# Attention's product of probabilities and values in four 32-column groups of the array, partial sums added when y is read

## The reference

```python
q = _apply_rope(q, cos, sin); k = _apply_rope(k, cos, sin)
scores = jnp.einsum('bhqd,bhkd->bhqk', q, k) / jnp.sqrt(jnp.asarray(hd, x.dtype))
scores = jnp.where(causal, scores, jnp.asarray(-jnp.inf, x.dtype))
attn = jax.nn.softmax(scores, axis=-1)
y = jnp.einsum('bhqk,bhkd->bhqd', attn, v)
...
return jnp.einsum('btc,oc->bto', y, w_proj)
```

## Time and profile before

| | |
|---|---|
| time, median of 3 runs | 3512.9 us (3508.41 to 3513.11) |
| span of the profiled execution, first to last instruction | 3506.6 us |
| loop over heads within it | from about 2785 to 3316 us |
| period of a head in the steady state | 16.00 us (3003.76 to 3019.76) |
| mean granted clock of TensorE, whole span | 0.954 |

### The profile page before, as it was taken

How to read it: one execution, slowest core, us unless ns; L and a number is a source line. 1 busy time by engine, 2 the same in 40 slices (tenths; PEclk the granted TensorE clock), 3 DMA queues, 4 the chain that set the end, 5 groups by cost and what they waited for, 6 DMA issues and landing times. The chain is left out here.

```text
span 3506.6 us, 40196 instructions
## 1 busy us (share of the span) xinstructions
PE 3137.1 (89%) x11856; PEld 1686.1 (48%) x11856; DVE 2278.1 (65%) x3726; ACT 1005.0 (29%) x2369; POOL 660.5 (19%) x441
## 2 busy tenths in 40 slices
PE   2899899988989989899898998988799799999989
PEld 1444454444544445444454454544684433333368
DVE  4777777777777777776777767665546455555354
ACT  1322323223232232232222322322213233333321
POOL 1122122122222212212222221222210000000021
PEclk7899999999999999999999999998899899999999
DMA  5000010010010001001001100000104100000000
GB/s 169 13 22 4 25 49 13 1 65 19 4 59 25 4 25 50 13 1 65 19 4 56 28 4 19 33 0 1 64 0 166 50 28 22 27 22 27 9 7 18
DMA packets 48126, 107.68 MB, mean 31 GB/s; under 512 B 9104, under 2 KB 18400, under 8 KB 45248
## 3 DMA queue, kind: packets, MB, share of 16 engines
q1 hardware_dynamic: 42624, 102.47, 8.8%
q10 hardware_dynamic: 5312, 2.92, 0.3%
HBM read 86.23 MB, written 19.14 MB: 30 GB/s over the span
## 5 line engine op out<-in xcount | busy, mean ns | idle before, releaser
L439 PE MATMUL bank<-xnT,wh 128*128 128x512 f32 x1280 | 592.4, 607 | 124.4 <-DVE sg L842 92.2
L528 PE MATMUL bank<-wg,xnT 128*128 128x512 f32 x1024 | 482.3, 615 | 0.0
L580 PE MATMUL bank<-wo,ggT 128*128 128x512 f32 x1024 | 466.0, 609 | 0.5 <-ACT ggT L689 0.5
L439 PEld LDWEIGHTS bank<-xnT,wh 128*128 128x128 f32 x1280 | 241.2, 194 | 410.8 <-issue 278.1
L733 DVE SCALAR_TENSOR_TENSOR cacc<-raw,cwh,cacc 128x512 f32<-128x512 f32 x480 | 390.3, 813 | 17.0
L580 PEld LDWEIGHTS bank<-wo,ggT 128*128 128x128 f32 x1024 | 201.7, 198 | 237.7 <-issue 232.3
L1821 PE MATMUL bank<-at_PT,at_vz 128*49 128x512 f32 (+3 forms) x768 | 298.5, 499 | 0.8 <-ACT at_yTs L1890 0.8
L528 PEld LDWEIGHTS bank<-wg,xnT 128*128 128x128 f32 x1024 | 193.4, 199 | 197.3 <-issue 197.3
L1914 DVE TENSOR_REDUCE at_nm<-bank 128x1 f32<-128x512 f32 (+3 forms) x256 | 151.1, 591 | 206.4 <-PE bank L1783 161.8
L503 PEld LDWEIGHTS bank<-xch,em 128*128 128x128 f32 x2048 | 237.4, 194 | 55.2 <-issue 52.2
L503 PE MATMUL bank<-xch,em 128*128 128x64 f32 x2048 | 243.5, 278 | 6.4 <-DVE em L791 2.4
(11 more groups left out here) (243 smaller groups left out, 4655.3 us busy)
## 6 DMA issues: line engine op xcount, KB each, us to landing
wh<-w_hs_dram SPq DMA_DIRECT2D x80, 256.0 KB, 2.7
wg<-w_gate_dram SPq DMA_DIRECT2D x8, 2048.0 KB, 7.7
wo<-w_out_dram SPq DMA_DIRECT2D x8, 2048.0 KB, 8.7
qk_scratch<-at_part SPq DMA_DIRECT2D x48, 256.0 KB
at_qT<-qk_scratch SPq DMA_DIRECT2D x32, 192.0 KB, 2.6
at_kT<-qk_scratch SPq DMA_DIRECT2D x32, 192.0 KB, 2.6
pk<-pack_scratch SPq DMA_DIRECT2D x16, 272.0 KB, 3.1
wgu<-w_gu_dram SPq DMA_DIRECT2D x1, 3584.0 KB, 11.3
```

Source lines behind the costliest of these rows:

```text
L439: mm = nc.tensor.matmul(BA[bank][:, :], wh[:, j, k, :], xnT[:, k, h * HALF:(h + 1) * HALF], start=(k == 0), stop=(k == KC - 1))
L528: mm = nc.tensor.matmul(BA[b][:, :], xnT[:, k, ttok], wg[:, k, u * 512:(u + 1) * 512], start=(k == 0), stop=(k == KC - 1))
L580: mm = nc.tensor.matmul(BA[b][:, :], ggT[:, j, :], wo[:, j, :], start=(j == 0), stop=(j == JT - 1))
```

## The change

`vz` loses its zeros on the left: it holds 17 columns and 15 of zeros, and the stationary operand has 32 columns. Each of the 12 products is written to one of four groups of 32 partitions of `BYT` (g = 0 to 3), which are four groups of 32 columns of the array. Groups 0, 1 and 2 share the products of b = 1, group 3 has those of b = 0. ScalarE copies all 128 partitions, the transposes bring all four groups along, and VectorE adds the three partial sums of b = 1 when it reads them. The products stand in three runs of four, behind `s1(., 2)`, `s1(., 4)` and `s1(., 6)`; nothing of them is left behind `s1(., 7)` or `m_rows`.

```diff
-            vz = sb(c1, "at_vz", [P, 2, NT, VZ + AD + 1 + VZ])
+            vz = sb(c1, "at_vz", [P, 2, NT, VZ])
             yT_ = sb(c1, "at_yTs", [P, T // 2])
+            yp = sb(c1, "at_yp", [P, NT, AD + 1])
...
-                    nc.gpsimd.memset(yT_[:, :], 0.0).then_inc(s_set, 1)
-                    pool.wait_ge(s_set, 4)
+                    pool.wait_ge(s_set, 3)
...
-                            lo = 0 if b else VZ
-                            mm = nc.tensor.matmul(BYT[0:VZ + AD + 1, 512 - n:], vz[:, r, j, lo:lo + VZ + AD + 1], PT_[:, r, c:c + n],
-                                                  start=((b, j) == PV1[0]), stop=((b, j) == PV3[-1]))
+                            mm = nc.tensor.matmul(BYT[VZ * g:VZ * (g + 1), 512 - n:], vz[:, r, j, :], PT_[:, r, c:c + n],
+                                                  start=((g, b, j) in OPENS), stop=((g, b, j) in ENDS))
...
-                    PV1 = [(1, 0), (1, 7), (1, 6), (1, 5), (1, 4), (1, 3)]
-                    PV2 = [(1, 2), (1, 1)]
-                    PV3 = [(0, 0), (0, 1), (0, 2), (0, 3)]
-                    AMONG = {1: 0, 2: 1, 3: 2, 4: 3, 5: 4, 6: 5}
+                    PV1 = [(0, 1, 0), (1, 1, 1), (2, 1, 3), (3, 0, 0)]
+                    PV2 = [(0, 1, 5), (1, 1, 2), (2, 1, 4), (3, 0, 1)]
+                    PV3 = [(0, 1, 6), (1, 1, 7), (3, 0, 2), (3, 0, 3)]
+                    OPENS = PV1
+                    ENDS = [(0, 1, 6), (1, 1, 7), (2, 1, 4), (3, 0, 3)]
+                    AMONG = {2: PV1, 4: PV2, 6: PV3}
...
                             if before and i in AMONG:
-                                b, j = PV1[AMONG[i]]
-                                pv(h - 1, 1 - r, b, [j])
+                                pv(h - 1, 1 - r, AMONG[i])
...
-                        if before:
-                            for b, j in PV2:
-                                pv(h - 1, 1 - r, b, [j])
                         if not last:
                             m_rows(h + 1, 1 - r)
-                        if before:
-                            for b, j in PV3:
-                                pv(h - 1, 1 - r, b, [j])
...
-                        nc.scalar.copy(yT_[0:VZ + AD + 1, :], BYT[0:VZ + AD + 1, :]).then_inc(a_y.sem, 1)
+                        nc.scalar.copy(yT_[:, :], BYT[:, :]).then_inc(a_y.sem, 1)
...
-                        ps = BM[:, :].rearrange("p (i s d) -> p s i d", i=NT // 2, s=P // VZ)[:, 0:2]
-                        nc.vector.reciprocal(ri[:, :].rearrange("p (s i) -> p s i", s=2), ps[:, :, :, AD]).then_inc(v_ri.sem, 1)
-                        v_ri.wait(dve, h + 1)
-                        nc.vector.tensor_tensor(halves(yo[:, :, :]), ps[:, :, :, 0:AD],
-                                                halves(ri[:, :].unsqueeze(2).broadcast_to([P, NT, AD])), ALU.mult).then_inc(v_y.sem, 1)
+                        ps = BM[:, :].rearrange("p (i s d) -> p i s d", i=NT // 2, s=P // VZ)
+                        nc.vector.tensor_copy(yp[:, 0:NT // 2, :], ps[:, :, 3, 0:AD + 1]).then_inc(v_ri.sem, 1)
+                        nc.vector.tensor_reduce(yp[:, NT // 2:, :], ps[:, :, 0:3, 0:AD + 1].rearrange("p i s d -> p i d s"),
+                                                AX, ALU.add).then_inc(v_ri.sem, 1)
+                        v_ri.wait(dve, 3 * h + 2)
+                        nc.vector.reciprocal(ri[:, :], yp[:, :, AD]).then_inc(v_ri.sem, 1)
+                        v_ri.wait(dve, 3 * h + 3)
+                        nc.vector.tensor_tensor(yo[:, :, :], yp[:, :, 0:AD],
+                                                ri[:, :].unsqueeze(2).broadcast_to([P, NT, AD]), ALU.mult).then_inc(v_y.sem, 1)
```

More of the change, by code:

```diff
@@ L1758, in _ @@
                     nc.gpsimd.memset(vz[:, :, :, :], 0.0).then_inc(s_set, 1)
-                    nc.gpsimd.memset(yT_[:, :], 0.0).then_inc(s_set, 1)
-                    pool.wait_ge(s_set, 4)
+                    pool.wait_ge(s_set, 3)
                     def take(h, r):
                         t_pv.wait(pool, h - 1)
-                        nc.gpsimd.tensor_copy(vz[:, r, :, VZ:VZ + AD + 1], V[:, :, bass.ds(h, 1), :].rearrange("p z o d -> p z (o d)"))\
+                        nc.gpsimd.tensor_copy(vz[:, r, :, 0:AD + 1], V[:, :, bass.ds(h, 1), :].rearrange("p z o d -> p z (o d)"))\
                             .then_inc(po_v.sem, 1)
@@ L1808, in m_rows, with pv @@
                         mm.then_inc(t_m.sem, 1)
-                    def pv(h, r, b, js):
-                        for j in js:
-                            if (b, j) == PV1[0]:
+                    def pv(h, r, blocks):
+                        for g, b, j in blocks:
+                            if (g, b, j) == PV1[0]:
                                 po_v.wait(pe, h + 1)
@@ L1819, in pv @@
                             c = OFF[j] + q0_ - j * P
-                            lo = 0 if b else VZ
-                            mm = nc.tensor.matmul(BYT[0:VZ + AD + 1, 512 - n:], vz[:, r, j, lo:lo + VZ + AD + 1], PT_[:, r, c:c + n],
-                                                  start=((b, j) == PV1[0]), stop=((b, j) == PV3[-1]))
-                            if (b, j) == PV3[-1]:
+                            mm = nc.tensor.matmul(BYT[VZ * g:VZ * (g + 1), 512 - n:], vz[:, r, j, :], PT_[:, r, c:c + n],
+                                                  start=((g, b, j) in OPENS), stop=((g, b, j) in ENDS))
+                            if (g, b, j) == PV3[-1]:
                                 mm.then_inc(t_pv.sem, 1)
-                    PV1 = [(1, 0), (1, 7), (1, 6), (1, 5), (1, 4), (1, 3)]
-                    PV2 = [(1, 2), (1, 1)]
-                    PV3 = [(0, 0), (0, 1), (0, 2), (0, 3)]
-                    AMONG = {1: 0, 2: 1, 3: 2, 4: 3, 5: 4, 6: 5}
+                    PV1 = [(0, 1, 0), (1, 1, 1), (2, 1, 3), (3, 0, 0)]
[4 more added lines that the diff above has]
+                    AMONG = {2: PV1, 4: PV2, 6: PV3}
                     def turn(h):
@@ L1854, in body @@
                             if before and i in AMONG:
-                                b, j = PV1[AMONG[i]]
-                                pv(h - 1, 1 - r, b, [j])
+                                pv(h - 1, 1 - r, AMONG[i])
                             if i == 2 and (not isinstance(h, int) or h >= 2):
                                 turn(h - 2)
-                        if before:
-                            for b, j in PV2:
-                                pv(h - 1, 1 - r, b, [j])
                         if not last:
                             m_rows(h + 1, 1 - r)
-                        if before:
-                            for b, j in PV3:
-                                pv(h - 1, 1 - r, b, [j])
                     def last(h, r):
                         body(h, r, True)
-                        for b, j in PV1 + PV2 + PV3:
-                            pv(h, r, b, [j])
+                        pv(h, r, PV1 + PV2 + PV3)
                         turn(h - 1)
@@ L1900, in last @@
                         take_y(h)
-                    act.wait_ge(s_set, 4)
+                    act.wait_ge(s_set, 3)
                     heads(act, None, body, last, (a_ex, a_y))
@@ L1933, in output @@
                         t_y.wait(dve, h + 1)
-                        ps = BM[:, :].rearrange("p (i s d) -> p s i d", i=NT // 2, s=P // VZ)[:, 0:2]
-                        halves = lambda ap: ap.rearrange("p (s i) d -> p s i d", s=2)
-                        nc.vector.reciprocal(ri[:, :].rearrange("p (s i) -> p s i", s=2), ps[:, :, :, AD]).then_inc(v_ri.sem, 1)
-                        v_ri.wait(dve, h + 1)
-                        nc.vector.tensor_tensor(halves(yo[:, :, :]), ps[:, :, :, 0:AD],
-                                                halves(ri[:, :].unsqueeze(2).broadcast_to([P, NT, AD])), ALU.mult).then_inc(v_y.sem, 1)
+                        ps = BM[:, :].rearrange("p (i s d) -> p i s d", i=NT // 2, s=P // VZ)
[7 more added lines that the diff above has]
+                                                ri[:, :].unsqueeze(2).broadcast_to([P, NT, AD]), ALU.mult).then_inc(v_y.sem, 1)
                         v_y.wait(dve, 2 * h + 1)
```

## The result

The changed kernel takes 3531.9 us (median of 4 runs, 3528.2 to 3535.3) against 3512.6 us before (median of 4 runs too): 1.0058 of the time, with a 95% interval of 1.0043 to 1.0072. It is slower, as forecast, but by 19 us and not by 67. Its profiled execution has a span of 3533.0 us.

The account below looks back on a forecast made before the run. TensorE sets the period, with a latency chain covered by products. A head of 16.7 us plus 1.6 for the clock is 18.3, against 16.00; 31 x 2.3 = +71, less 2.8 and 1.7, gives +67: 3580 us, range 3500 to 3630.

Parts of the forecast that it names:

- What bounds the kernel: Steady head: TensorE, busy 15.58 of 16.00 us, sets the period, plus a VectorE latency chain at the end covered by products.
- the price of a product: Single product between scores: 1.14 us, of which 0.853 product, about 0.06 mask matmul, 0.23 way in and out.
- the bubble: Head's end, last s1 to next s2: 4.03 us chain through VectorE, bare of products after the change.
- The waits behind it: TensorE behind VectorE's longer output: 0.42 us for s1(3)'s maximum, 0.7 us for s1(4)'s maxima and two banks.
- What the groups give: A head's three runs of products: 4.90 us in place of 7.68, bounds 2.35 and 7.68.
- staircase: Within a run, only one product's second pass overlaps the next's first: four 512-column products take 5 passes, 2.13 us.
- Rival 1: All four products of a run abreast, clock drops partly hidden: 16.3 us a head, 3515 us; chance 0.18.
- The clock: At bare head ends granted clock drops to 1.2 GHz in 8 of 10, 2.0 us each: 1.6 us a head.
- rival 3: Two-pass staircase as forecast, no clock drops: 16.7 us a head, 3530 us; chance 0.13.
- The order's price: Per head, 3.0 us of bubble that held products and 1.6 us of stalls, outweighing gains of 2.78 and 1.15 us.
- The signs: Whole kernel's time: chance of faster by over 0.2% 0.17, same 0.07, slower 0.76.
- The ways in and out: Around each run of products TensorE pays 0.23 us once; the range allowed for this doubled, 3545 to 3610 us.

Follow-up runs that it names:

- e1_busy_end: Changed kernel with ten idle bfloat16 matmuls of 512 columns ahead of the 8 transposes at each head's end: 3466.1 us, 0.9873 of before.
- e9_pairs_adjacent: e1_busy_end with products of one group placed next to each other in the first two runs of products: 3498.7 us, 0.9962 of before.
- e3_new_order_49: Kernel before with only its products reordered into the changed kernel's three runs of four, 49 columns wide, no groups: 3664.3 us, 1.0431 of before.
- e6: Changed kernel with second and third runs of products back at the head's end and VectorE's output moved earlier: 3401.9 us, 0.9689 of before.
- e2_runs_at_end: Changed kernel with second and third runs of products moved back to the head's end, around the transposes: 3479.9 us, 0.9909 of before.
- e8_end_early_busy: e6 plus five idle bfloat16 matmuls of 512 columns between the second run of products and the 8 transposes: 3414.9 us, 0.9721 of before.

## Why the prediction failed, point by point

**What bounds the kernel, the price of a product, the bubble: right.** The end of the head without products was put at 4.03 us and is 4.10 (3014.94 to 3019.04). The output on VectorE was put at 1.55 us and takes 1.42 (3009.61 to 3011.03 in this trace). The waits behind it were put at 0.42 and 0.7 us, and are 0.29, 0.41 and 0.45. The wait for the exponentials was put at 0.5 us and is 0.45 in e1_busy_end, at full clock.

**What the groups give: wrong, and this is the step that failed.** "The trace shows matmuls start in program order, never one ahead of another" was true of a trace in which the products share columns of the array (all 76 matmuls of the head from 3003.76 stand in program order), and it cannot tell what happens when they don't. I took 4.90 us for the products of a head. No run shows this staircase or its 4.90 us; the runs show 2.35 in streams: in e1_busy_end, at full clock, the three runs take 1.00, 0.99 and 0.78 us from their start to the next matmul (3005.93 to 3006.93, 3009.20 to 3010.19, 3012.83 to 3013.61), of which 0.14 each is the way out. e9_pairs_adjacent shows what happens in its place: only a matmul's own group held it back. 2.55 us a head, 79 us over 31 heads, is more than the whole error of 48 us. The lower bound of 2.35 us stood in the text; the choice between the bounds went by the wrong row. Rival 1, a run at the cost of its widest product, was nearer to what happens: the four groups here, in float32, give 3.2 times (3.14 us in e3_new_order_49 for 0.99). Across groups matmuls do not start strictly in order: in e9 the first product of one group begins with the first of the other (3008.32 and 3008.31), ahead of three passes that stand before it.

**The clock: right in kind, too small in size.** I read head 0 as the model of every head and took a fall in 8 of 10, 1.6 us a head. It falls in every head of the profiled stretch, and e1 measures what it costs: 17.07 - 14.82 = 2.25 us a head, 66 us in all. This undid a part of the first error, and the sum can be redone: from the forecast head of 18.3 us, 2.55 us less of products, 0.7 more of waits and 0.65 more by the clock give 17.1, and 17.07 was measured. Over 31 heads that is 38 of the 48 us; of the other 10 the last head makes 5.5, put at 2.8 us of gain and measured at 8.3. At full clock the head was predicted at 14.8 us if the groups run side by side; e1 has 14.82 (3003.38 to 3018.20).

**So after is rival 1, whose place was right and whose number was not**: 14.8 us and a fall, put at 16.3 us and 3515 us since I thought a part of the fall hidden in waits for VectorE; it is 17.07 and 3532. That rival 3 stood at 3530 is chance: its period of 16.7 us had the staircase and no falls, and neither is in the trace.

**The order's price** of "3.0 us of bubble that held products and 1.6 us of stalls" can be read off the runs: e3, the order alone, is 152 us; moving the two runs back and the output out of the way (e6) takes 130 us from the changed kernel.

**The signs**: slower by over 0.2% had 0.76 (the chances of the rivals, added up, give 0.79) and came true. The time lies in the range of 3500 to 3630, but the loss was forecast three and a half times too large, and the cause is the staircase.

**The ways in and out.** The second run of after lasts 0.99 us to the next s2 and 0.85 of them are its widest product, which leaves 0.14 us for the way out; the way in is the 0.15 us from the mask matmul at 3009.82 less its own 0.06. Together 0.23 us, as for the 49 columns before. So the ways in and out are no dearer for groups of 32 columns; no run shows them doubled, as the upper part of the range had them.

## What to carry to other kernels

Products with a narrow stationary operand can go into different column groups of the array. Here, with 32 columns and float32, four that stood next to each other in the program ran side by side (0.99 us for 3.14). Where one stood alone between other matmuls (0.98 us for 0.99), or where TensorE waited anyway (0.85 us less of products, 0.85 us more of wait), groups gave nothing. When such a change makes TensorE's work shorter, ask in the same step what the removed work had covered: a chain through another engine, waits for a bank, and the clock itself. Keep real work in the gap, and put the other engine's long operation where that engine waits. Look for the place where the clock falls before filling a gap: idle work in the bare end gave 66 us, and cost 13 us where the falls began ahead of it.

## What was not expected of the hardware

- Passes of different column groups started out of program order: four first passes within 0.02 us of the run's start at 3009.97, ahead of second passes that stand before them and begin at 3010.32 or later; a run took as long as its fullest group (0.99 us for 384, 512, 512, 384 columns; 1.84 us for two groups of 1024 and 896 columns; 3.14 us without groups).
- Adding 2.2 us of idle matmuls to each head made the kernel 66 us faster, by the granted clock alone (0.80 to 1.00).
- The clock fell not only where TensorE stood still: in e2_runs_at_end it fell where TensorE was busy 0.95 of 2.90 us between waits. In e6_end_early_out it fell behind a stretch in which TensorE was busy 2.64 of 3.80 us. Why it falls in some heads of e6_end_early_out and e8_end_early_busy and not in others of the same program stays open.
